# Attention in a one-core kernel: row sums by matmuls with ones behind the values product, in place of normalised probabilities

## The chip, the cores and the metric

The kernel runs on one core of one Trainium2 chip. A core has five engines with a queue each: TensorE (PE; its weight loads are PEld), VectorE (DVE), ScalarE (ACT), GpSimd (POOL) and SyncE (SP, which only issues transfers here). The metric is the time of one execution on the device, in microseconds; lower is better.

## The reference

Four blocks on an input of 16 images of 28 x 28 pixels with 32 channels, each behind a group normalisation with a residual: windowed attention, a state-space block, a triangle product and a recurrent net. The change touches the first. Cut to what matters:

```python
win = x.reshape(B, nH, 7, nW, 7, C)...reshape(-1, 49, C)     # 256 windows of 49 pixels
qkv = win @ w_qkv + b_qkv                                     # 4 heads of 8 channels
attn = einsum('whnd,whmd->whnm', q, k) * scale
attn = softmax(attn, axis=-1)
out = einsum('whnm,whmd->whnd', attn, v)
out = out @ w_proj + b_proj
```

## The kernel before, in words

The 128 partitions hold four image groups (g, 32 channels each). Pixels lie along the free axis and are cut into 16 strips of 7 rows, 196 pixels, that is four windows of 49. A strip goes through attention in a software pipeline, and each engine has a function that writes one turn s of it: `pe_att`, `act_att`, `dve_att` and `pool_att`. Turns run from -1 to 17; the middle ones are loops of two turns. Every engine works in its own order, and semaphores join them: `x_r` counts finished instructions of kind x.

In turn s of the kernel before:

- TensorE: scores of strip s in two halves of two groups (L1150), queries and keys of strip s+1 (L1165, L1166), four groups of transposes of strip s-1's probabilities (L1193), the projection of strip s-2 (L1175), values of strip s+1 (L1234), the product of probabilities and values of strip s-1 (L1204, "values product").
- VectorE: for each half of the scores of strip s the row maxima (L1814) and their subtraction (L1820); the residual addition of strip s-2 (L1826); the row sums of the four groups (L1832) with two reciprocals (L1836).
- ScalarE: queries and keys out of PSUM (L701, L706), transposed blocks out of PSUM (L715) alternating with the exponentials (L724), values (L746), the values product out of PSUM with the bias of the values (L755).
- GpSimd: the strip of input by windows (L469), the keys masked by head (L474), and the multiplication of the four groups of exponentials by the reciprocals (L480), for which the transposes wait (`pn_r`).

Transposed blocks and values share two banks of PSUM in turn (`ring_r`); the values product has bank 7, queries, keys and projection share bank 4.

Behind turn 10 VectorE takes the statistics of the first two images, behind turn 11 ScalarE takes a logarithm and an exponential for their normalisation, and behind turn 12 VectorE writes them into padded images. On TensorE the first convolution of the state-space block comes between turns 15 and 16, and pieces of that block stand between, and behind, the parts of turns 16 and 17 (`early`, `late`); on VectorE turn 17 stands behind the block's first instruction (L1879).

Of the kernel before, what the change touches and what calls it, by code (L numbers as in the profile page):

```python
# [8 lines left out]
ALU = mybir.AluOpType  # L9
# [29 lines left out]
def build(nc, a, out):  # L39
    ctx = ExitStack()  # L40
    with ctx:
# [26 lines left out]
        epsc = sb("epsc", [P, 1])  # L68
        early_ln = sb("early_ln", [P, 1])
        negone = sb("negone", [P, 1])  # L70
        vec = sb("vec", [P, 16])
# [46 lines left out]
        mx = sb("mx", [P, G, 8], att)  # L118
        sm = sb("sm", [P, G, 8], att)
        rc = sb("rc", [P, G, 8], att)  # L120
        att.close()
# [88 lines left out]
        qk_d, v_r, s_r, t_r, av_r, pj_r, q_r, k_r, exp_r, ring_r = sems("qk_d v_r s_r t_r av_r pj_r q_r k_r exp_r ring_r")  # L210
        xw_r, km_r, pn_r, max_r, sub_r, sum_r, rec_r, ao_r, x1_r = sems("xw_r km_r pn_r max_r sub_r sum_r rec_r ao_r x1_r")

# [28 lines left out]
        def windows(ap):  # L241

            return ap.rearrange("p (r w c) -> p w r c", r=WS, w=NW)

        def bcast(ap, axis, n):
# [186 lines left out]
        def _(eng):  # L432
# [27 lines left out]
            def pool_att(s, par):  # L460
                nxt = not isinstance(s, int) or s + 1 < NS
                cur = not isinstance(s, int) or s >= 0
                np_ = 1 - par
                if nxt:
# [197 lines left out]
        def _(eng):  # L662
# [28 lines left out]
            def act_att(s, par, before_output=None):  # L691
# [3 lines left out]
                prv = not fixed or 1 <= s <= NS  # L695
                np_ = 1 - par
                if nxt:
# [11 lines left out]
                def turned_out(g):  # L709
                    if not prv:  # L710
                        return
                    eng.wait_ge(t_r, 4 * (s - 1) + g + 1)
                    if g == 0 and (not fixed or s >= 2):
                        eng.wait_ge(av_r, s - 1)
                    eng.activation(PT[:, g].rearrange("p a b (o q) -> p (a b o) q", o=2),  # L715
                                   banks[5 + (par + 1 + g) % 2][:, :].rearrange("p (m k) -> p m k", k=WP)[:, :, 0:WT], ACT.Copy).then_inc(ring_r, 1)

                def exponent(g):
                    if not cur:
                        return  # L720
                    eng.wait_ge(sub_r, 4 * s + g + 1)
                    if not fixed or s >= 2:
                        eng.wait_ge(t_r, 4 * (s - 2) + g + 1)
                    eng.activation(Pr[:, par, g, :, 0:WT], Ts[:, g, :, :], ACT.Exp).then_inc(exp_r, 1)  # L724
# [390 lines left out]
        def _(eng):  # L1115
# [13 lines left out]
            def pe_att(s, par, early=None, late=None):  # L1129
# [25 lines left out]

                scores(0)
                scores(1)
                if nxt:
                    if fixed and s < 0:
                        eng.wait_ge(s_xn, J)  # L1160
                    else:
                        eng.wait_ge(k_r, s + 1)
                    if not fixed or s >= 3:
                        eng.wait_ge(x1_r, s - 2)
                    eng.matmul(banks[4][:, 0:ST], BD[:, U_Q, :], XN[:, strip(s + 1)], start=True, stop=True)  # L1165
                    eng.matmul(banks[4][:, ST:2 * ST], BD[:, U_K, :], XN[:, strip(s + 1)], start=True, stop=True).then_inc(qk_d, 1)  # L1166

                def project():
# [12 lines left out]
                def transposes(g):  # L1181
                    eng.wait_ge(pn_r, 4 * (s - 1) + g + 1)

# [12 lines left out]
                def av():  # L1196
# [4 lines left out]
                    for w in range(NW):  # L1201
                        for e in range(2):
                            for g in range(G):
                                ins = eng.matmul(banks[7][C * g:C * g + C, WT * w:WT * w + WT], Vst[:, np_, w % 2, w // 2, g, e, :],  # L1204
                                                 PT[:, g, w // 2, e, WT * (w % 2):WT * (w % 2) + WT],
                                                 start=(e == 0), stop=(e == 1))
                    ins.then_inc(av_r, 1)

                if prv:
                    transposes(0)  # L1210
                    transposes(1)
                if early:
                    early()
# [7 lines left out]
                if fixed and s < 0:  # L1221

                    eng.wait_ge(s_v, TRB)
                    for g in range(G):
                        rows = slice(C * g, C * g + C)
                        eng.matmul(banks[7][rows, 0:C], NB[0:R, 17, :], TB[0:R, 16, :], start=True, stop=True)
                        ins = eng.matmul(banks[7][rows, C:C + 1], wzn[:, :], lnb[:, :], start=True, stop=True)
                    ins.then_inc(s_wd, 1)
                if nxt:
# [468 lines left out]
        def _(eng):  # L1698
# [8 lines left out]
            eng.memset(negone[:, :], -1.0)  # L1707
            eng.memset(epsc[:, :], EPS).then_inc(s_ev, 1)

            for j in range(0, J, 2):  # L1710
# [92 lines left out]
            def dve_att(s, par):  # L1803
# [4 lines left out]
                np_ = 1 - par  # L1808
                if cur:
                    for part in range(2):  # L1810
                        groups = (2 * part, 2 * part + 1)
                        eng.wait_ge(s_r, 2 * s + part + 1)
                        for g in groups:
                            eng.tensor_reduce(mx[:, g, :], banks[g][:, 0:392].rearrange("p (m k) -> p m k", k=WT), AX.X,  # L1814
                                              ALU.max).then_inc(max_r, 1)
                        for g in groups:
                            eng.wait_ge(max_r, 4 * s + g + 1)
                            if not fixed or s >= 1:
                                eng.wait_ge(exp_r, 4 * (s - 1) + g + 1)
                            eng.tensor_tensor(Ts[:, g, :, :], banks[g][:, 0:392].rearrange("p (m k) -> p m k", k=WT),  # L1820
                                              bcast(mx[:, g, :], 2, WT), ALU.subtract).then_inc(sub_r, 1)
# [5 lines left out]
                if cur:  # L1827
                    for g in range(G):
                        eng.wait_ge(exp_r, 4 * s + g + 1)
                        if not fixed or s >= 1:  # L1830
# [399 lines left out]
```

## Time and profile before

| what | value |
|---|---|
| three runs | 471.02, 473.19, 474.92 us; median 473.19 us |
| profiled execution, span from first to last instruction | 473.1 us |
| instructions | 10122 |
| busy: PE, PEld, DVE, ACT, POOL | 358.7, 233.1, 366.5, 299.2, 233.8 us |
| DVE's maxima of turn 0 to those of turn 15 | 31.75 to 139.26 us |

The page gives no time of the profiled execution beside its span; the span stands here for it, and it is 0.1 us from the median of the runs. Busy time is summed over stages that have different limits, so it doesn't say which engine sets the end in attention. In a timeline, a line gives the start, the time from the start of the first to the end of the last instruction merged into it, engine, line, operation, destination and sources, the number of instructions, and in brackets how long the engine sat idle before it and what it waited for.

### The profile page before, as it was taken

Reading aid. Unit: us, or ns where it says so; the run is one execution under the profiler, and the core shown is the slowest. Engines: PE = TensorE matmul, PEld = TensorE weight load, DVE = VectorE, ACT = ScalarE, POOL = GpSimd, SP = SyncE. Lnnn points to the kernel's source line nnn. Section 1 sums busy time; section 2 is a strip of 40 time slices with the busy share of each in tenths; the row PEclk is TensorE's granted clock in tenths of the full one; section 3 lists DMA queues with packets and bytes.
Section 4 is the critical chain, followed back from the end, with each engine's and each line's share of the span. In section 5 each row is a group of like instructions: output and inputs, shape, how many; then the busy total and the mean of one; then the engine's idle time right before and its main releaser. Section 6 shows DMA issues by size and latency. Waiting matters only on the chain. (4 is left out here: it accounts for less than half of the span.)

```text
span 473.1 us, 10122 instructions
## 1 busy us (share of the span) xinstructions
PE 358.7 (76%) x3531; PEld 233.1 (49%) x3531; DVE 366.5 (77%) x679; ACT 299.2 (63%) x583; POOL 233.8 (49%) x217
## 2 busy tenths in 40 slices
PE   4159888896789785996767565567797989888885
PEld 4047666675665432142223222122295549877774
DVE  4799999999697388789698899999575895544443
ACT  4327788887785899568775976344996354333432
POOL 4527868775663224964893799587162240000000
PEclk9557999998899999588898896766999999999999
DMA  6110000000222231013000000000002000111111
GB/s 148 5 18 3 4 0 0 0 0 1 55 63 66 55 86 31 1 35 82 1 0 1 0 1 0 0 0 1 1 10 62 0 1 11 20 19 22 21 19 26
DMA packets 24045, 10.31 MB, mean 22 GB/s; under 512 B 20576, under 2 KB 22368, under 8 KB 24016
## 3 DMA queue, kind: packets, MB, share of 16 engines
q1 hardware_dynamic: 23888, 9.93, 10.3%
q8 instruction: 16, 0.26, 0.2%
q0 software_dynamic: 128, 0.01, 0.2%
q14 instruction: 13, 0.11, 0.1%
HBM read 2.00 MB, written 1.61 MB: 8 GB/s over the span
## 5 line engine op out<-in xcount | busy, mean ns | idle before, releaser
L480 POOL TENSOR_TENSOR Pr<-Pr,rc 128x392 f32<-128x392 f32 x64 | 54.3, 881 | 32.5 <-DVE rc L1836 32.5
L511 POOL TENSOR_TENSOR YA<-YA,hC 128x784 f32<-128x784 f32 x27 | 52.8, 1956 | 34.4 <-DVE hC L1920 33.3
L1349 PE MATMUL pair<-BCf,sel 96*128 96x392 bf16 x128 | 38.0, 391 | 32.4 <-DVE Hs L1904 28.9
L1904 DVE TENSOR_TENSOR_SCAN Hs<-dA,pair 128x784 f32<-128x784 f32 x32 | 57.1, 1785 | 1.0
L1193 PE MATMUL pair<-ident,Pr 128*128 128x128 f32 x256 | 41.3, 294 | 13.2 <-ACT PT L715 8.7
L1349 PEld LDWEIGHTS pair<-BCf,sel 96*128 96x128 bf16 x128 | 10.3, 104 | 71.8 <-issue 70.2
L1193 PEld LDWEIGHTS pair<-ident,Pr 128*128 128x128 f32 x256 | 29.5, 147 | 25.1 <-ACT PT L715 15.9
L1897 DVE TENSOR_TENSOR pair<-DU,pair 128x784 f32<-128x784 f32 x32 | 31.2, 974 | 10.9 <-PE pair L1349 10.5
L715 ACT ACTIVATE PT<-pair 128x392 f32<-128x392 f32 x64 | 31.3, 496 | 6.2 <-PE pair L1193 5.9
L724 ACT ACTIVATE Pr<-Ts 128x392 f32<-128x392 f32 x64 | 32.5, 536 | 3.3 <-DVE Ts L1820 3.2
L1814 DVE TENSOR_REDUCE mx<-pair 128x8 f32<-128x392 f32 x64 | 32.6, 551 | 1.3 <-PE pair L1150 1.0
L1646 PE MATMUL pair<-hst,BD 128*128 128x112 f32 x168 | 25.7, 289 | 10.1 <-DVE hst L2193 9.2
L1820 DVE TENSOR_TENSOR Ts<-pair,mx 128x392 f32<-128x392 f32 x64 | 32.9, 555 | 0.0
L846 ACT ACTIVATE dA<-DL,Aneg 128x784 f32<-128x784 f32 x32 | 29.0, 940 | 5.2 <-DVE Hs L1904 5.1
L1832 DVE TENSOR_REDUCE sm<-Pr 128x8 f32<-128x392 f32 x64 | 31.9, 538 | 0.3 <-ACT Pr L724 0.3
L2180 DVE SCALAR_TENSOR_TENSOR prods<-gates 128x112 f32<-128x112 f32 x28 | 7.7, 276 | 31.5 <-ACT gates L1100 31.5
L1100 ACT ACTIVATE gates<-pair 128x224 f32<-128x224 f32 x28 | 10.0, 357 | 33.7 <-PE pair L1646 33.7
L474 POOL TENSOR_TENSOR Km<-Ks,mask 128x784 f32<-128x784 f32 x16 | 24.1, 1505 | 11.9 <-ACT Ks L706 11.9
L1920 DVE TENSOR_TENSOR hC<-Hs,pair 128x784 f32<-128x784 f32 x27 | 25.7, 951 | 3.3 <-PE pair L1349 3.2
L1646 PEld LDWEIGHTS pair<-hst,BD 128*128 128x128 f32 x168 | 20.9, 191 | 14.7 <-DVE hst L2193 14.3
L1287 PE MATMUL pair<-SX,W 96*32 96x392 f32 x192 | 22.7, 588 | 6.1 <-ACT BCf L815 5.6
L746 ACT ACTIVATE Vst<-pair 64x128 f32<-64x128 f32 x64 | 17.3, 271 | 15.1 <-PE pair L1204 8.6
(262 smaller groups left out, 943.2 us busy)
## 6 DMA issues: line engine op xcount, KB each, us to landing
SX<-XP SPq DMA_DIRECT2D x48, 112.2 KB
XT<-in_x SPq DMA_DIRECT2D x4, 392.0 KB, 5.1
out<-Os SPq DMA_DIRECT2D x28, 56.0 KB, 1.8
AD<-Aa SPq DMA_DIRECT2D x4, 196.0 KB
NB<-in_L_conv_x_proj_w SPq DMA_DIRECT2D x4, 3.0 KB
DW<-in_L_conv_dw SPq DMA_DIRECT2D x4, 1.1 KB
vec<-in_L_conv_b_qkv POOLq DMA_DIRECT2D x3, 0.5 KB, 5.8
W<-in_L_conv_w_qkv SPq DMA_DIRECT2D x1, 48.0 KB
```

Of the source, the lines that this page charges most:

```text
L480: eng.tensor_tensor(pg, pg, bcast(rc[:, g, :], 2, WT), ALU.mult).then_inc(pn_r, 1)
L511: eng.tensor_tensor(y, y, hC[:, n % NHC, :], ALU.add).then_inc(g_ya, 1)
L715: eng.activation(PT[:, g].rearrange("p a b (o q) -> p (a b o) q", o=2), banks[5 + (par + 1 + g) % 2][:, :].rearrange("p (m k) -> p m k", k ...
L724: eng.activation(Pr[:, par, g, :, 0:WT], Ts[:, g, :, :], ACT.Exp).then_inc(exp_r, 1)
L1193: ins = eng.transpose(bk[:, P * k:P * k + P], pg, ident[:, :])
L1349: ins = eng.matmul(SPREAD[s][:, columns(h)], sel[:, n, :], upper(BCf[:, c % 2, s, columns(h)]), start=True, stop=True)
L1646: ins = eng.matmul(zb[k], BD[:, U_M + k, :], hst[:, 1 - par, :], start=False, stop=True, skip_group_check=True)
L1814: eng.tensor_reduce(mx[:, g, :], banks[g][:, 0:392].rearrange("p (m k) -> p m k", k=WT), AX.X, ALU.max).then_inc(max_r, 1)
L1820: eng.tensor_tensor(Ts[:, g, :, :], banks[g][:, 0:392].rearrange("p (m k) -> p m k", k=WT), bcast(mx[:, g, :], 2, WT), ALU.subtract).then_ ...
L1832: eng.tensor_reduce(sm[:, g, :], Pr[:, par, g, :, 0:WT], AX.X, ALU.add).then_inc(sum_r, 1)
L1897: eng.tensor_tensor(SPREAD[0], DU[:, c % 2, :], SPREAD[0], ALU.mult).then_inc(v_b, 1)
L1904: eng.tensor_tensor_scan(Hs[:, n % 2, :], dA[:, n % NA, :], SPREAD[0], 0.0, ALU.mult, ALU.add).then_inc(v_s, 1)
```

## The change

The exponentials are transposed as they are. Behind the values product of strip s-1 TensorE multiplies the same transposed blocks by a matrix of ones (`ones`, set up at the start), which gives each pixel's sum of exponentials, per head, in the other half of bank 7, laid out as the values product is. VectorE inverts these 128x196 sums (`den`) and multiplies them into the values product on its way out of PSUM, one turn later (`attended`). That takes the place of VectorE's row sums and small reciprocals, GpSimd's multiplications and ScalarE's eviction of the values product. The bias of the values goes through the projection into the projection's bias, once at the start. The order within a turn changes as well: on TensorE the first group of transposes stands ahead of the scores, the second behind them and ahead of queries and keys; on ScalarE the first two transposed blocks stand ahead of queries and keys, and the exponentials behind all four blocks; on VectorE `attended` stands between the two halves of maxima and subtractions.

```diff
@@ pool_att
-                if cur:
-                    for g in range(G):
-                        eng.wait_ge(rec_r, 2 * s + g // 2 + 1)
-                        pg = Pr[:, par, g, :, 0:WT]
-                        eng.tensor_tensor(pg, pg, bcast(rc[:, g, :], 2, WT), ALU.mult).then_inc(pn_r, 1)
@@ act_att
+                turned_out(0)
+                turned_out(1)
                 if nxt:
                     eng.wait_ge(qk_d, s + 2)
...
-                turned_out(0)
-                exponent(0)
-                turned_out(1)
-                exponent(1)
                 turned_out(2)
                 turned_out(3)
-                exponent(2)
-                exponent(3)
+                for g in range(G):
+                    exponent(g)
...
-                if prv:
-                    eng.wait_ge(av_r, s)
-                    if not fixed or s >= 3:
-                        eng.wait_ge(pj_r, s - 2)
-                    eng.activation(windows(AO[:, np_, :]), banks[7][:, 0:ST].rearrange("p (w r c) -> p w r c", w=NW, r=WS),
-                                   ACT.Identity, bias=vec[:, V_BV:V_BV + 1]).then_inc(ao_r, 1)
@@ pe_att
                 def transposes(g):
-                    eng.wait_ge(pn_r, 4 * (s - 1) + g + 1)
+                    eng.wait_ge(exp_r, 4 * (s - 1) + g + 1)
...
                     ins.then_inc(av_r, 1)
+                    if fixed and s == 1:
+                        eng.wait_ge(ones_r, 3)
+                    for e in range(2):
+                        for g in range(G):
+                            ins = eng.matmul(banks[7][C * g:C * g + C, 256:256 + ST], ones[:, e, :], PT[:, g, :, e, :],
+                                             start=(e == 0), stop=(e == 1))
+                    ins.then_inc(sum_r, 1)
 
                 if prv:
                     transposes(0)
+                scores(0)
+                scores(1)
+                if prv:
                     transposes(1)
+                if nxt:
...
+                    eng.matmul(banks[4][:, 0:ST], BD[:, U_Q, :], XN[:, strip(s + 1)], start=True, stop=True)
+                    eng.matmul(banks[4][:, ST:2 * ST], BD[:, U_K, :], XN[:, strip(s + 1)], start=True, stop=True).then_inc(qk_d, 1)
                 if early:
                     early()
@@ setup
+            eng.memset(ones[:, :, :], 0.0).then_inc(ones_r, 1)
+            eng.wait_ge(ones_r, 1)
+            for u in range(2):
...
+                eng.memset(heads, 1.0).then_inc(ones_r, 1)
...
+                    eng.matmul(banks[7][:, C + 1:C + 2], BD[:, U_P, :], vec[:, V_BV:V_BV + 1], start=True, stop=True).then_inc(s_wd, 1)
...
+            eng.tensor_tensor(vec[:, V_BP:V_BP + 1], vec[:, V_BP:V_BP + 1], banks[7][:, C + 1:C + 2], ALU.add)
@@ dve_att
+                def attended():
+
+                    eng.wait_ge(sum_r, s - 1)
+                    eng.reciprocal(den[:, :], banks[7][:, 256:256 + ST]).then_inc(rec_r, 1)
+                    eng.wait_ge(rec_r, s - 1)
+                    eng.tensor_tensor(windows(AO[:, par, :]), by_window(banks[7][:, 0:ST]),
+                                      by_window(den[:, :]), ALU.mult).then_inc(ao_r, 1)
+
+                shifted(0)
                 if prv2:
-
+                    attended()
+                shifted(1)
+                if prv2:
                     eng.wait_ge(pj_r, s - 1)
                     xs = X[:, strip(s - 2)]
                     eng.scalar_tensor_tensor(xs, banks[4][:, 0:ST], vec[:, V_BP:V_BP + 1], xs, ALU.add, ALU.add).then_inc(x1_r, 1)
-                if cur:
-                    for g in range(G):
-                        eng.wait_ge(exp_r, 4 * s + g + 1)
-                        if not fixed or s >= 1:
-                            eng.wait_ge(pn_r, 4 * (s - 1) + g + 1)
-                        eng.tensor_reduce(sm[:, g, :], Pr[:, par, g, :, 0:WT], AX.X, ALU.add).then_inc(sum_r, 1)
-                        if g >= 2:
-                            lo = 2 * (g - 2)
-                            eng.wait_ge(sum_r, 4 * s + lo + 2)
-                            eng.reciprocal(rc[:, lo:lo + 2, :], sm[:, lo:lo + 2, :]).then_inc(rec_r, 1)
```

`shifted(part)` is the former first loop of `dve_att` for one half, unchanged: wait for that half of the scores, two maxima, two subtractions. The projection (`project`) is unchanged: it waits for `ao_r` to reach s-1, which `attended` of the same turn now counts; so does the values product, as before.

## Rows read from the trace of the kernel before

**Rows 1.** Busy time by stage: length, then each engine, then PEclk, DMA.

```profile
68.00:101.00 33.00, 29.78 (x610) 22.79 (x610) 32.09 (x76) 28.09 (x76) 24.68 (x30) 1.00 0.00 0
```

**Rows 2.** Timeline of VectorE in attention and behind it.

```profile
44.50 1.04 DVE L1814 TENSOR_REDUCE mx<-pair 128x8 f32<-128x392 f32 x2 [0.20 <-PE pair L1150]
...
58.30 1.04 DVE L1814 TENSOR_REDUCE mx<-pair 128x8 f32<-128x392 f32 x2 [0.53 <-PE pair L1150]
...
91.98 1.04 DVE L1814 TENSOR_REDUCE mx<-pair 128x8 f32<-128x392 f32 x2
...
93.89 1.03 DVE L1814 TENSOR_REDUCE mx<-pair 128x8 f32<-128x392 f32 x2
...
96.22 1.49 DVE L1832 TENSOR_REDUCE sm<-Pr 128x8 f32<-128x392 f32 x3
...
98.49 0.99 DVE L1814 TENSOR_REDUCE mx<-pair 128x8 f32<-128x392 f32 x2
...
114.36 1.04 DVE L1814 TENSOR_REDUCE mx<-pair 128x8 f32<-128x392 f32 x2
...
126.39 1.02 DVE L1814 TENSOR_REDUCE mx<-pair 128x8 f32<-128x392 f32 x2
...
139.26 0.97 DVE L1814 TENSOR_REDUCE mx<-pair 128x8 f32<-128x392 f32 x2
...
162.66 1.62 DVE L1879 SCALAR_TENSOR_TENSOR sp<-sp 128x784 f32<-128x784 f32 x1 [7.73 <-ACT sp L823]
```

**Rows 3.** Timeline of ScalarE behind turn 11 and at attention's end.

```profile
115.22 1.28 ACT L771 ACT_TABLE_LOAD   x1
...
118.23 0.41 ACT L701 ACTIVATE Qw<-pair,vec 128x196 f32<-128x196 f32 x1
...
157.77 0.44 ACT L755 ACTIVATE AO<-pair,vec 128x196 f32<-128x196 f32 x1 [0.28 <-PE pair L1204]
...
165.01 0.82 ACT L815 ACTIVATE BCf<-pair 96x784 f32<-96x784 f32 x1
```

**Rows 4.** Timeline of TensorE in attention.

```profile
57.34 0.95 PE L1150 MATMUL pair<-Km,Qw 32*64 32x196 f32 x32
...
90.65 1.11 PE L1150 MATMUL pair<-Km,Qw 32*64 32x196 f32 x32 [0.37 <-issue]
...
92.46 1.18 PE L1193 MATMUL pair<-ident,Pr 128*128 128x128 f32 x8
...
95.22 0.50 PE L1175 MATMUL pair<-AO,BD 128*128 128x196 f32 x2
95.56 0.69 PE L1234 MATMUL pair<-BD,xw 128*128 128x128 f32 x4
96.18 0.91 PE L1204 MATMUL pair<-PT,Vst 128*32 128x49 f32 x64
97.02 0.95 PE L1150 MATMUL pair<-Km,Qw 32*64 32x196 f32 x32
...
109.77 1.12 PE L1193 MATMUL pair<-ident,Pr 128*128 128x128 f32 x4 [1.93 <-ACT PT L715]
...
144.01 4.13 PE L1287 MATMUL pair<-SX,W 96*32 96x392 f32 x48
```

**Rows 5.** The page's costliest groups: count, busy us, mean ns, idle before.

```profile
L480 POOL TENSOR_TENSOR Pr<-Pr,rc 128x392 f32<-128x392 f32 x64 | 54.3, 881 | 32.5 <-DVE rc L1836 32.5
...
L1820 DVE TENSOR_TENSOR Ts<-pair,mx 128x392 f32<-128x392 f32 x64 | 32.9, 555 | 0.0
```

**Rows 6.** Reciprocals by line: duration ns min/median/max, first and last start.

```profile
L1836 DVE RECIPROCAL rc<-sm x32: 234/248/254, 36.9 to 145.5; 128x16 f32<-128x16 f32 x32
...
L2099 DVE RECIPROCAL zst<-zst x4: 271/317/319, 367.6 to 373.0; 128x28 f32<-128x28 f32 x4
...
L1951 DVE RECIPROCAL rstd<-lnv x3: 156/157/164, 324.4 to 343.1; 128x1 f32<-128x1 f32 x2, 128x2 f32<-128x2 f32 x1
```

**Rows 7.** Busy time in half microseconds where TensorE had idled; PEclk third from the end.

```profile
109.50:110.00 0.50, 0.23 (x1) 0.23 (x2) 0.50 (x2) 0.50 (x2) 0.08 (x1) 0.50 0.00 0
```

More of the change, by code:

```diff
@@ L69, in build @@
         early_ln = sb("early_ln", [P, 1])
+        ones = sb("ones", [P, 2, C])
         negone = sb("negone", [P, 1])
@@ L118, in build @@
         mx = sb("mx", [P, G, 8], att)
-        sm = sb("sm", [P, G, 8], att)
-        rc = sb("rc", [P, G, 8], att)
+        den = sb("den", [P, ST], att)
         att.close()
@@ L210, in build @@
         qk_d, v_r, s_r, t_r, av_r, pj_r, q_r, k_r, exp_r, ring_r = sems("qk_d v_r s_r t_r av_r pj_r q_r k_r exp_r ring_r")
-        xw_r, km_r, pn_r, max_r, sub_r, sum_r, rec_r, ao_r, x1_r = sems("xw_r km_r pn_r max_r sub_r sum_r rec_r ao_r x1_r")
+        xw_r, km_r, max_r, sub_r, sum_r, ln_r, rec_r, ao_r, x1_r, ones_r = sems("xw_r km_r max_r sub_r sum_r ln_r rec_r ao_r x1_r ones_r")
         PRODUCTS = "conv x2 u z delta xB xC out var wout".split()
@@ L243, in windows, with by_window @@
             return ap.rearrange("p (r w c) -> p w r c", r=WS, w=NW)
+        def by_window(ap):
+            return ap.rearrange("p (v y c) -> p v y c", v=NW, y=WS)
         def bcast(ap, axis, n):
@@ L461, in pool_att @@
                 nxt = not isinstance(s, int) or s + 1 < NS
-                cur = not isinstance(s, int) or s >= 0
                 np_ = 1 - par
@@ L696, in act_att, with turned_out, exponent @@
                 np_ = 1 - par
+                def turned_out(g):
+                    if not prv:
+                        return
+                    eng.wait_ge(t_r, 4 * (s - 1) + g + 1)
+                    if g == 0 and (not fixed or s >= 2):
+                        eng.wait_ge(sum_r, s - 1)
+                    eng.activation(PT[:, g].rearrange("p a b (o q) -> p (a b o) q", o=2),
+                                   banks[5 + (par + 1 + g) % 2][:, :].rearrange("p (m k) -> p m k", k=WP)[:, :, 0:WT], ACT.Copy).then_inc(ring_r, 1)
+                def exponent(g):
+                    if not cur:
+                        return
+                    eng.wait_ge(sub_r, 4 * s + g + 1)
+                    if not fixed or s >= 2:
+                        eng.wait_ge(t_r, 4 * (s - 2) + g + 1)
+                    eng.activation(Pr[:, par, g, :, 0:WT], Ts[:, g, :, :], ACT.Exp).then_inc(exp_r, 1)
+                turned_out(0)
+                turned_out(1)
                 if nxt:
@@ L708, in act_att @@
                                    bias=vec[:, V_BK:V_BK + 1]).then_inc(k_r, 1)
[L709 to L724, printed above, removed]
-                turned_out(0)
-                exponent(0)
-                turned_out(1)
-                exponent(1)
                 turned_out(2)
                 turned_out(3)
-                exponent(2)
-                exponent(3)
+                for g in range(G):
+                    exponent(g)
                 if nxt:
@@ L1154, in scores @@
                     ins.then_inc(s_r, 1)
[L1156 to L1166, printed above, removed]
                 def project():
@@ L1207, in av @@
                     ins.then_inc(av_r, 1)
+                    if fixed and s == 1:
[5 more added lines that the diff above has]
+                    ins.then_inc(sum_r, 1)
                 if prv:
                     transposes(0)
+                scores(0)
+                scores(1)
+                if prv:
                     transposes(1)
+                if nxt:
+                    if fixed and s < 0:
+                        eng.wait_ge(s_xn, J)
+                    else:
+                        eng.wait_ge(k_r, s + 1)
+                    if not fixed or s >= 3:
+                        eng.wait_ge(x1_r, s - 2)
+                    eng.matmul(banks[4][:, 0:ST], BD[:, U_Q, :], XN[:, strip(s + 1)], start=True, stop=True)
+                    eng.matmul(banks[4][:, ST:2 * ST], BD[:, U_K, :], XN[:, strip(s + 1)], start=True, stop=True).then_inc(qk_d, 1)
                 if early:
@@ L1226, in pe_att @@
                         eng.matmul(banks[7][rows, 0:C], NB[0:R, 17, :], TB[0:R, 16, :], start=True, stop=True)
-                        ins = eng.matmul(banks[7][rows, C:C + 1], wzn[:, :], lnb[:, :], start=True, stop=True)
-                    ins.then_inc(s_wd, 1)
+                        eng.matmul(banks[7][rows, C:C + 1], wzn[:, :], lnb[:, :], start=True, stop=True)
+                    eng.matmul(banks[7][:, C + 1:C + 2], BD[:, U_P, :], vec[:, V_BV:V_BV + 1], start=True, stop=True).then_inc(s_wd, 1)
                 if nxt:
@@ L1708, in _ @@
             eng.memset(epsc[:, :], EPS).then_inc(s_ev, 1)
+            eng.memset(ones[:, :, :], 0.0).then_inc(ones_r, 1)
+            eng.wait_ge(ones_r, 1)
+            for u in range(2):
+                half = ones[64 * u:64 * u + 64]
+                heads = bass.AP(half.tensor, half.offset + HD * u, [list(half.ap[0]), [C + 2 * HD, 2], [1, HD]])
+                eng.memset(heads, 1.0).then_inc(ones_r, 1)
             for j in range(0, J, 2):
@@ L1808, in dve_att, with shifted @@
                 np_ = 1 - par
-                if cur:
[L1810 to L1817, printed above, removed]
-                            if not fixed or s >= 1:
-                                eng.wait_ge(exp_r, 4 * (s - 1) + g + 1)
-                            eng.tensor_tensor(Ts[:, g, :, :], banks[g][:, 0:392].rearrange("p (m k) -> p m k", k=WT),
-                                              bcast(mx[:, g, :], 2, WT), ALU.subtract).then_inc(sub_r, 1)
+                def shifted(part):
+                    if not cur:
+                        return
+                    groups = (2 * part, 2 * part + 1)
+                    eng.wait_ge(s_r, 2 * s + part + 1)
+                    for g in groups:
+                        eng.tensor_reduce(mx[:, g, :], banks[g][:, 0:392].rearrange("p (m k) -> p m k", k=WT), AX.X,
+                                          ALU.max).then_inc(max_r, 1)
+                    for g in groups:
+                        eng.wait_ge(max_r, 4 * s + g + 1)
+                        if not fixed or s >= 1:
+                            eng.wait_ge(exp_r, 4 * (s - 1) + g + 1)
+                        eng.tensor_tensor(Ts[:, g, :, :], banks[g][:, 0:392].rearrange("p (m k) -> p m k", k=WT),
+                                          bcast(mx[:, g, :], 2, WT), ALU.subtract).then_inc(sub_r, 1)
+                def attended():
+                    eng.wait_ge(sum_r, s - 1)
+                    eng.reciprocal(den[:, :], banks[7][:, 256:256 + ST]).then_inc(rec_r, 1)
[6 more added lines that the diff above has]
+                shifted(1)
                 if prv2:
@@ L1826, in dve_att @@
                     eng.scalar_tensor_tensor(xs, banks[4][:, 0:ST], vec[:, V_BP:V_BP + 1], xs, ALU.add, ALU.add).then_inc(x1_r, 1)
-                if cur:
-                    for g in range(G):
-                        eng.wait_ge(exp_r, 4 * s + g + 1)
-                        if not fixed or s >= 1:
-                            eng.wait_ge(pn_r, 4 * (s - 1) + g + 1)
-                        eng.tensor_reduce(sm[:, g, :], Pr[:, par, g, :, 0:WT], AX.X, ALU.add).then_inc(sum_r, 1)
-                        if g >= 2:
-                            lo = 2 * (g - 2)
-                            eng.wait_ge(sum_r, 4 * s + lo + 2)
-                            eng.reciprocal(rc[:, lo:lo + 2, :], sm[:, lo:lo + 2, :]).then_inc(rec_r, 1)
             for s in (0, 1, 2):
```

## The prediction

> **What bounds the kernel now.** I read the stage table first, then VectorE's timeline of one turn, then TensorE's, then the few places where attention is not in its steady turn. The stage table [rows 1] shows VectorE busy 32.09 of 33.00 us in the steady part of attention, TensorE 29.78, ScalarE 28.09 and GpSimd 24.68. VectorE's timeline says the same in detail: within a turn (maxima, subtractions, residual, row sums, reciprocals) each instruction starts as the one before ends, and the next turn's maxima follow with hardly a gap; turn 9 runs from 91.98 to 98.49, 6.51 us [rows 2]. So in the steady turns VectorE is the bound, and the row sums with their reciprocals, 96.22 to 98.49, are 2.27 us of it. TensorE spends that time on the values product and the next scores, so it has the next maxima's input ready about when VectorE comes free.
>
> Two stretches differ. The turn that starts at 114.36 takes 12.03 us, because ScalarE loads activation tables from 115.22 until its next query eviction at 118.23 [rows 2, 3]. And attention's end releases the rest: the first convolution starts on TensorE at 144.01, straight after the last steady turn [rows 4], and the state-space part starts from that. I therefore take a shift of attention's end as a shift of the whole.
>
> **What is removed.** Of VectorE, 2.27 us a turn (four sums, two reciprocals). Of GpSimd, 64 multiplications of 881 ns [rows 5]: they sat between the sums and the transposes, and GpSimd is not the bound; without them the transposes need the exponentials alone, which a turn earlier are long done. Of ScalarE, one eviction of 0.44 us a turn [rows 3]; ScalarE has room.
>
> **What is added.** (a) The reciprocal of 128x196. No row has one so long. Reciprocals of 16 elements take 248 ns, of 28 elements 317, of one or two 157 [rows 6]: 317 - 248 over 12 is 5.8 ns an element, 248 - 157 over 14 is 6.5. I take 6.0 ns on 248 for 16: 0.248 + 180 x 0.0060 = 1.33 us. The ends: 7.0 ns (156 to 254 over 14 elements) gives 1.51 us; a plain instruction's rate, a 128x392 subtraction in 555 ns [rows 5] and so half its elements in some 0.36, is the floor. I stand near the first, since it is the same operation.
>
> The Trainium skill ("VectorE: DVE Perf Modes", section "Walkthrough: the 8-slice pipeline in each mode") says that the reciprocal is an iterative divide with a repeat count of 8. Read as eight cycles an element at the page's 0.96 GHz that is an estimate of 8.3 ns, 1.75 us for 196 elements, and would put the total 6 us above mine; the rows' 5.8 to 6.5 ns do not bear that out.
>
> (b) The multiplication of 128x196: half the elements of a subtraction, 0.36 us. It waits for the reciprocal's end, 0.05 more. VectorE's new step is 1.33 + 0.05 + 0.36 = 1.74 us.
>
> (c) The matmuls with ones: eight of 196 columns into four column groups. The values product in front has 32 of 49 columns into the same groups, so as many columns (1568), and holds TensorE from 96.18 to 97.02, 0.84 us [rows 4]; with an eighth to a quarter of the weight loads I take 0.75, between 0.5 and 0.84. If the groups did not overlap it were sixteen passes of some 0.17 (a projection, two passes, holds TensorE 0.34, 95.22 to 95.56), 2.7 us. It can't be below zero: the work is new.
>
> Setup: one memset with its two strips at the start, where VectorE waits for x, one 128x1 addition, one one-column matmul: 0.2 us together, inside the rounding.
>
> **What is moved, and the loop that it closes.** VectorE's total per turn falls: 6.51 - 2.27 + 1.74 = 5.98 us. But the new step stands between the two halves of the maxima, and on TensorE the projection, in order, waits for it; behind the projection are queued the next values (V), the values product, the sums, the first transposes and only then the next scores; and for those scores VectorE's next maxima wait, before which the next new step cannot come. Before, the projection's input came from ScalarE at the end of the turn before, and no such round existed. It, once a turn:
>
> - start of scores to the first maximum: 57.34 to 58.30 with VectorE idle, 0.96 [rows 2, 4];
> - both maxima and subtractions of the first half: 91.98 to 93.89, 1.91;
> - reciprocal and multiplication, 1.74;
> - hand-over to TensorE with the projection's weight load, 0.15 (estimate; TensorE's hand-overs in these rows are that or more);
> - projection, V, values product: 95.22 to 97.02, 1.80;
> - sums, 0.75;
> - the first transposes, now ahead of the scores: two groups take 1.18 [rows 4], of which a matmul's own latency is part; 0.55.
>
> Sum 7.86 us, against 5.98 of VectorE's work. TensorE then idles about a microsecond before each projection and VectorE nearly two before the scores come. I checked the other rounds: keys to mask to scores (GpSimd's mask, no longer queued behind multiplications), and ScalarE's order (transposed blocks, queries, keys, blocks, four exponentials, values) end earlier than this one.
>
> **The sum.** Turns 2 to 14, from the maxima at 44.50 to those at 139.26, took 94.76 us [rows 2]. After: 13 x 7.86 = 102.2; six loop boundaries at which TensorE idles 0.37 [rows 4], now on the round, 2.2; the statistics after turn 10 0.3 (2.2 us of them into 1.9 of slack); the two table loads 0.4, because ScalarE's 3 us now fall where the projection waits anyway. Together 105.1, +10.3 us. Turns 0 and 1: VectorE is lighter by the sums, but TensorE at 1.2 GHz does transposes and sums more before the next scores: worked out at the rows' durations, +0.6. End of the last steady turn: 144.01 - 139.26 = 4.75 before; after, 1.91 + 1.74 + 0.15 + 0.34 + 0.84 + 0.75 = 5.7, +1.0. The tail: ScalarE's last output eviction at 157.77 with 0.28 of idle before it falls away, -0.7 [rows 3]; but the last new step is queued on VectorE behind the instruction at 162.66 (1.62 us) of the state-space part, and the last projection, the product that ScalarE evicts at 165.01 and the second convolution are queued behind it on TensorE: 162.63 + 1.67 + 1.74 + 0.15 + 0.34 + 1.5 (that product) = 168.0, +3.0 [rows 2, 3]. Net +2.3.
>
> 0.6 + 10.3 + 1.0 + 2.3 = +14.2 us. The profiled execution's span, 473.1, agrees with the median of 473.19, so I put the sum on the median: 487. By the bounds: the reciprocal at 1.11 or 1.51 moves it by -3 or +3 (15 times), the sums at 0.5 or 0.84 by -4 or +1, the hand-overs and the tail by some 3 either way. Own range 478 to 497.
>
> **Rivals.**
> 1. The reciprocal costs like any other instruction, 0.36. The round shrinks by 0.97 in 15 turns: 487 - 14.6 = 472.5, no change. Against it: rows 6. Chance 0.10.
> 2. Faster: the round does not bind, and VectorE stays the bound. It turns on the round being under VectorE's 6 us: that takes a reciprocal of 0.36 and another microsecond less, as where the first half of the scores releases the maxima after 0.5 (not 0.96, which the rows show with both halves in flight) and the sums hide half their time. Then turns of 6.2 and loop boundaries give 13 x 6.2 + 2.2 + 0.7 = 83.5, -11.2, with the other terms at +1: 463. Chance 0.07.
> 3. TensorE's clock falls. Before, TensorE idled 1.93 us up to 109.77, and the granted clock went from 1.00 to 0.50 (2.4 to 1.2 GHz) at that point; one group of transposes there took 1.12 us, where two take 1.18 at the full clock [rows 1, 4, 7]. The changed kernel idles about 1 us in every turn; shorter gaps left the clock alone before. If half of the turns fell to 1.2 GHz behind the wait, each would pay about 1.5 us more: 487 + 10 = 497. Chance 0.13; matmuls with ones that don't overlap (+27) are in it with 0.02.
>
> **How the numbers follow.** The forecast has 0.70, with the rivals 0.10, 0.07 and 0.13. 1% is 4.7 us, about what a measurement of this kernel can tell from no change. Slower by more: nearly all of the forecast and of rival 3, 0.80. Within: rival 1 and the forecast's low edge, 0.12. Faster: 0.08, rival 2 and rival 1's low edge. The range takes the forecast's own and reaches down to the edge of rival 1 and up to rival 3: 474 to 498.
>
> **What would show it.** VectorE's instruction on a 128x196 reciprocal at 1.1 to 1.5 us. Turns of 7.6 to 8.2 us in place of 6.7. The projection waiting on VectorE's multiplication, about 1 us a turn, as TensorE's longest wait, and VectorE's first maxima waiting for the scores, near 2 us. VectorE's busy share in this stage down to about three quarters. The convolution starting some 12 us later, with the state-space part unchanged but for its start. It would be wrong if the reciprocal runs at plain speed, or if the turn is shorter than the sum of its round, which would mean that a hand-over is sooner than the rows show.

## The result and the profile after

The changed kernel takes 482.91 us (median of five, 482.28 to 486.42) where the kernel before took 473.19 beside it (five, 470.89 to 474.92): a ratio of 1.024 [1.019, 1.028], 9.7 us slower. The forecast was 487 in a range of 474 to 498, with 0.80 on slower. The profiled execution of the changed kernel is the slowest of its five: 486.42 us at a span of 483.5; the spans of the others are 480.1 to 481.6. Positions below are those of that profile.

The stage table over the same stretch of attention as [rows 1] (same columns):

```profile
68.00:101.00 33.00, 25.64 (x562) 20.48 (x560) 25.15 (x48) 22.86 (x61) 7.68 (x9) 1.00 0.00 0
```

Every engine is less busy than before, VectorE 25.15 us in place of 32.09, and yet less attention is done in these 33 us. No engine bounds this stretch any more. One turn on VectorE, from the timeline (start, busy us, line, names, count, and in brackets the idle time ahead and what ended it); it answers to the turn in [rows 2]:

```profile
67.01 1.04 DVE L1818 TENSOR_REDUCE mx<-pair 128x8 f32<-128x392 f32 x2 [1.93 <-PE pair L1138]
67.96 1.03 DVE L1824 TENSOR_TENSOR Ts<-pair,mx 128x392 f32<-128x392 f32 x2
68.91 1.38 DVE L1830 RECIPROCAL den<-pair 128x196 f32<-128x196 f32 x1
70.32 0.36 DVE L1832 TENSOR_TENSOR AO<-pair,den 128x196 f32<-128x196 f32 x1
70.60 1.03 DVE L1818 TENSOR_REDUCE mx<-pair 128x8 f32<-128x392 f32 x2
71.54 1.03 DVE L1824 TENSOR_TENSOR Ts<-pair,mx 128x392 f32<-128x392 f32 x2
72.48 0.42 DVE L1842 SCALAR_TENSOR_TENSOR X<-pair,vec,X 128x196 f32 x1
74.83 1.04 DVE L1818 TENSOR_REDUCE mx<-pair 128x8 f32<-128x392 f32 x2 [1.93 <-PE pair L1138]
```

The same turn on TensorE, which answers to [rows 4]:

```profile
66.05 0.95 PE L1138 MATMUL pair<-Km,Qw 32*64 32x196 f32 x32
...
68.08 1.04 PE L1169 MATMUL pair<-ident,Pr 128*128 128x128 f32 x8
70.81 0.59 PE L1151 MATMUL pair<-AO,BD 128*128 128x196 f32 x2 [1.69 <-DVE AO L1832]
71.24 0.61 PE L1229 MATMUL pair<-BD,xw 128*128 128x128 f32 x4
71.78 0.91 PE L1180 MATMUL pair<-PT,Vst 128*32 128x49 f32 x64
72.51 0.84 PE L1188 MATMUL pair<-PT,ones 128*32 128x196 f32 x16
73.28 0.66 PE L1169 MATMUL pair<-ident,Pr 128*128 128x128 f32 x4
73.87 0.95 PE L1138 MATMUL pair<-Km,Qw 32*64 32x196 f32 x32
```

Read the two brackets together. VectorE stands idle 1.93 us until the scores (L1138) come; the scores are last in TensorE's queue; TensorE stands idle 1.69 us until VectorE's multiplication (L1832); and that multiplication is behind the first maxima, for which those scores are the input. Two engines wait for each other once a turn, 7.82 us from maxima to maxima. The table of waits over attention (engine, line, waited for: us in total, times, longest) has the two waits side by side:

```profile
PE pair L1151 <- DVE AO L1832: 20.3, 12, 1.8
DVE mx L1818 <- PE pair L1138: 20.3, 11, 1.9
```

### The profile page after: what moved, and what is told of

The parts are those of the page before. It is cut to its first block and busy times, and to the rows that moved or that the text cites. A ratio compares the mean times of both kernels' runs of the same rounds, so it can differ in the third digit from the quotient of the medians.

```text
span 483.5 us, 10400 instructions
## 1 busy us (share of the span) xinstructions
PE 361.7 (75%) x3789; PEld 236.9 (49%) x3789; DVE 352.2 (73%) x619; ACT 295.0 (61%) x567; POOL 179.1 (37%) x153
## 5 line engine op out<-in xcount | busy, mean ns | idle before, releaser
L508 POOL TENSOR_TENSOR YA<-YA,hC 128x784 f32<-128x784 f32 x27 | 51.7, 1914 | 32.8 <-DVE hC L1926 32.0
L1344 PEld LDWEIGHTS pair<-BCf,sel 96*128 96x128 bf16 x128 | 10.4, 104 | 71.5 <-issue 69.5
L709 ACT ACTIVATE Pr<-Ts 128x392 f32<-128x392 f32 x64 | 31.5, 549 | 20.3 <-DVE Ts L1824 20.3
L1169 PE MATMUL pair<-ident,Pr 128*128 128x128 f32 x256 | 37.8, 281 | 3.2 <-ACT PT L700 2.0
L1903 DVE TENSOR_TENSOR pair<-DU,pair 128x784 f32<-128x784 f32 x32 | 31.2, 974 | 10.3 <-PE pair L1344 9.8
L700 ACT ACTIVATE PT<-pair 128x392 f32<-128x392 f32 x64 | 30.1, 501 | 12.4 <-PE pair L1169 12.0
L1151 PE MATMUL pair<-AO,BD 128*128 128x196 f32 x32 | 9.9, 391 | 27.6 <-DVE AO L1832 27.6
L1282 PE MATMUL pair<-SX,W 96*32 96x392 f32 x192 | 23.7, 611 | 5.3 <-ACT BCf L803 5.3
L1629 PE MATMUL pair<-XN,BD 128*128 (+1 forms) x168 | 25.2, 287 | 1.8 <-ACT XN L1068 1.8
L493 POOL TENSOR_TENSOR BCf<-BCf 64x784 f32<-64x784 f32 x8 | 11.9, 1487 | 32.8 <-ACT BCf L803 32.8
```

What stands on the lines that cost most here:

```text
L508: eng.tensor_tensor(y, y, hC[:, n % NHC, :], ALU.add).then_inc(g_ya, 1)
L1169: ins = eng.transpose(bk[:, P * k:P * k + P], pg, ident[:, :])
L1344: ins = eng.matmul(SPREAD[s][:, columns(h)], sel[:, n, :], upper(BCf[:, c % 2, s, columns(h)]), start=True, stop=True)
L1629: eng.matmul(zb[k].rearrange("p (b n) -> p b n", b=J), BD[:, U_X + k, :], xt, start=False, stop=False, skip_group_check=True)
L1903: eng.tensor_tensor(SPREAD[0], DU[:, c % 2, :], SPREAD[0], ALU.mult).then_inc(v_b, 1)
```

## Experiments

The leading theory: the changed step costs time because of its place. It stands between the two halves of the maxima, and so closes the round; neither VectorE's total nor the matmuls with ones bound the turn by themselves. Its rival: the step's own work (a long reciprocal on VectorE, sixteen more matmuls on TensorE) is what costs, wherever it stands. All edits are made to the changed kernel.

**The product ahead of the maxima.** The same instructions, but the reciprocal and the multiplication are issued ahead of the first half instead of behind it.

```diff
-                shifted(0)
                 if prv2:
                     attended()
+                shifted(0)
                 shifted(1)
```

> Moves the reciprocal and the multiplication on VectorE ahead of both halves of the maxima; no work is taken away. Theory (the round through the scores, the first maxima, the reciprocal and the projection sets the turn, 7.82 us in the trace of the changed kernel): the projection no longer waits for this turn's maxima, TensorE's wait of 1.69 us goes, and the turn falls to TensorE's own work, 6.1 to 6.3 us; 14 turns by some 1.6 make it about 22 us faster than the changed kernel, about 461 us and below the kernel before. Rival (the added work itself, the matmuls with ones and the long reciprocal, costs the time): nothing is removed, so the time stays within 3 us of 483.

Measured: 465.11 us (461.82 to 467.41), 0.984 [0.978, 0.990] of the kernel before and 17.8 us under the changed one, with no instruction fewer. The turn is 6.23 us, reciprocal to reciprocal, on VectorE's timeline of this kernel:

```profile
62.85 1.38 DVE L1830 RECIPROCAL den<-pair 128x196 f32<-128x196 f32 x1 [0.34 <-PE pair L1188]
64.27 0.36 DVE L1832 TENSOR_TENSOR AO<-pair,den 128x196 f32<-128x196 f32 x1
64.55 1.03 DVE L1818 TENSOR_REDUCE mx<-pair 128x8 f32<-128x392 f32 x2
65.49 1.02 DVE L1824 TENSOR_TENSOR Ts<-pair,mx 128x392 f32<-128x392 f32 x2
66.44 1.02 DVE L1818 TENSOR_REDUCE mx<-pair 128x8 f32<-128x392 f32 x2
67.38 1.02 DVE L1824 TENSOR_TENSOR Ts<-pair,mx 128x392 f32<-128x392 f32 x2
68.33 0.41 DVE L1842 SCALAR_TENSOR_TENSOR X<-pair,vec,X 128x196 f32 x1
69.08 1.38 DVE L1830 RECIPROCAL den<-pair 128x196 f32<-128x196 f32 x1 [0.34 <-PE pair L1188]
```

The maxima no longer wait for scores: while VectorE inverts and multiplies, TensorE already does them. What is left of idle time is 0.34 us before the reciprocal, for the sums. What sets this turn is TensorE's own matmuls, which follow each other almost without a gap (stage table of this kernel):

```profile
68.00:101.00 33.00, 32.81 (x758) 25.69 (x754) 31.12 (x60) 28.50 (x76) 9.44 (x12) 1.00 0.00 0
```

So the rival falls: the same work in another place is faster than the kernel before. The time missed its expectation by 4 us, and the trace says where. In the turn with the table loads the reciprocals start at 107.74 and 117.81, 10.07 us apart, where that turn took 8.13 in the changed kernel: ScalarE's loads are on the path again, since nothing else waits there. TensorE's timeline of this kernel shows the wait for ScalarE's transposed block:

```profile
112.78 1.36 PE L1169 MATMUL pair<-ident,Pr 128*128 128x128 f32 x8 [2.33 <-ACT PT L700]
...
115.60 1.48 PE L1180 MATMUL pair<-PT,Vst 128*32 128x49 f32 x64
```

Behind it the granted clock is 0.82 over 112.50 to 114.00, after 1.00 over 107 to 113, and the values product takes 1.48 us instead of 0.91.

**The reciprocal and the multiplication left out.** One copy in their place, so the output stays unnormalised.

```diff
-                    eng.reciprocal(den[:, :], banks[7][:, 256:256 + ST]).then_inc(rec_r, 1)
-                    eng.wait_ge(rec_r, s - 1)
-                    eng.tensor_tensor(windows(AO[:, par, :]), by_window(banks[7][:, 0:ST]),
-                                      by_window(den[:, :]), ALU.mult).then_inc(ao_r, 1)
+                    eng.tensor_copy(windows(AO[:, par, :]), by_window(banks[7][:, 0:ST])).then_inc(ao_r, 1)
```

> Leaves out the reciprocal and the multiplication: the unnormalised values product is copied out of PSUM by VectorE in the same place (about 0.3 us in place of 1.77). The sums are still made and not used. Theory: the round shrinks by 1.4 to 1.5 us to some 6.35, about 20 us faster than the changed kernel. Rival (TensorE's added matmuls are what lengthens the turn): VectorE had 1.9 us of idle time in the turn already, so no more than 3 us.

Measured: 464.81 us (459.61 to 466.00), 0.980 [0.972, 0.988] of the kernel before. VectorE's timeline of this kernel:

```profile
62.54 1.04 DVE L1818 TENSOR_REDUCE mx<-pair 128x8 f32<-128x392 f32 x2 [1.93 <-PE pair L1138]
...
64.44 0.35 DVE L1830 COPY AO<-pair 128x196 f32<-128x196 f32 x1
...
68.94 1.04 DVE L1818 TENSOR_REDUCE mx<-pair 128x8 f32<-128x392 f32 x2 [1.93 <-PE pair L1138]
```

The turn is 6.40 us, shorter by 1.42: the reciprocal's 1.38 and its hand-over to the multiplication. VectorE idles 1.93 us as before. So in the changed place each microsecond of the reciprocal is a microsecond of the turn, although VectorE has room for it. The turn came out as expected (6.35); the time is 18.1 us under the changed kernel instead of about 20. The time lies near that of the product first by chance: there TensorE's matmuls set a turn of 6.23 us, here the round sets one of 6.40.

**More work for VectorE off the round.** Three row sums a turn (of the shifted scores) are put back on VectorE behind its last instruction of the turn, where it waits for scores. The sums are used nowhere.

```diff
...
+                if cur:
+                    for g in range(3):
+                        eng.wait_ge(sub_r, 4 * s + g + 1)
+                        eng.tensor_reduce(sm[:, g, :], Ts[:, g, :, :], AX.X, ALU.add)
```

> Puts three row sums of 128x392 (of the shifted scores, results unused) back on VectorE behind the residual addition, 1.45 us a turn. Theory: they fit into VectorE's idle 1.93 us before the next maxima, so the turn stays at 7.8 us and the time within 2 us of the changed kernel: the row sums that the change removed are worth nothing in its own turn. Rival (VectorE's work sets the turn in the changed kernel too): 14 times 1.45, 20 us slower.

In the steady turns this held: 7.82 us (maxima at 68.07 and 75.89) with 1.48 us more on VectorE a turn, taken from the 1.93 of idle. In VectorE's timeline of this kernel:

```profile
73.87 1.48 DVE L1847 TENSOR_REDUCE sm<-Ts 128x8 f32<-128x392 f32 x3
75.89 1.04 DVE L1819 TENSOR_REDUCE mx<-pair 128x8 f32<-128x392 f32 x2 [0.54 <-PE pair L1139]
...
112.97 1.48 DVE L1847 TENSOR_REDUCE sm<-Ts 128x8 f32<-128x392 f32 x3
114.38 1.96 DVE L1721 BATCH_NORM_STATS2 stats<-X 128x6 f32<-128x392 f32 x4
116.37 0.28 DVE L1862 BATCH_NORM_AGGREGATE mv<-stats 128x2 f32<-128x12 f32 x2
116.57 0.98 DVE L1819 TENSOR_REDUCE mx<-pair 128x8 f32<-128x392 f32 x2
...
118.42 1.37 DVE L1831 RECIPROCAL den<-pair 128x196 f32<-128x196 f32 x1
```

But the whole took 488.78 us (487.20 to 492.55), 5.9 more than the changed kernel against at most 2 expected. The lower lines show why: after turn 10 the statistics (2.2 us) follow, and with the sums ahead of them the slack of 1.93 is used twice. The next maxima start at 116.57 with no idle time ahead, and the reciprocal comes 9.35 us after the last one (109.07 to 118.42), where the changed kernel has 7.95. The late product then makes TensorE wait, in its timeline of this kernel:

```profile
120.31 1.01 PE L1152 MATMUL pair<-AO,BD 128*128 128x196 f32 x2 [3.22 <-DVE AO L1833]
```

The granted clock is 0.50 over 120.50 to 122.50, and the turn that follows takes 10.45 us (118.42 to 128.87) instead of 7.83. The same happens once more, smaller, before 139.16. Slack in the steady turn is not slack in every turn.

**The last product taken earlier.** Only the last product is moved on VectorE, ahead of the state-space part's instruction of 1.62 us (line 1885 of the changed kernel); the round stays as it is. `rest=False` leaves out the residual addition of the turn, `product=False` the reciprocal and the multiplication.

```diff
...
+            dve_att(17, 1, rest=False)
             eng.wait_ge(a_u, 1)
             eng.scalar_tensor_tensor(rest, sp[:, SP_U, :], 1.0, sp[:, SP_E, :], ALU.subtract, ALU.subtract).then_inc(v_cc, 1)
-            dve_att(17, 1)
+            dve_att(17, 1, product=False)
```

> Only the last strip's reciprocal and multiplication move, on VectorE, ahead of the state-space part's first instruction. Theory of the tail: TensorE's idle 5.46 us before the last projection falls to about 1, the projection and the product behind it run at full clock, and ScalarE's copy of that product no longer waits 4.77 us; 4 to 5 us faster at the first scan, of which 3 to 5 reach the end. Rival (the first scan waits for other work of the tail): under 1 us.

Measured: 477.61 us (475.87 to 479.28), 5.3 under the changed kernel. First the changed kernel, TensorE's timeline at the last product:

```profile
173.39 1.02 PE L1151 MATMUL pair<-AO,BD 128*128 128x196 f32 x2 [5.46 <-DVE AO L1832]
174.21 2.82 PE L1267 MATMUL pair<-US,WBC 128*96 128x392 f32 x4
```

and this kernel:

```profile
169.18 0.60 PE L1151 MATMUL pair<-AO,BD 128*128 128x196 f32 x2 [0.41 <-DVE AO L1832]
169.62 1.48 PE L1267 MATMUL pair<-US,WBC 128*96 128x392 f32 x4
```

Without the 5.46 us of waiting TensorE keeps its clock (1.00 over 169 to 172, where the changed kernel has 0.50 over 173.50 to 176.50), and the product for ScalarE's copy takes 1.48 us instead of 2.82. The copy itself starts at 173.21 instead of 177.12, and the first scan at 182.02 instead of 185.96. The profiled execution of this kernel is 1.06 us late before the edit comes into play (turn 15's maxima at 146.72 instead of 145.66), so from there the first scan comes 5.0 us sooner, 35.30 us in place of 40.30. The 5.3 us are a little more than the expected 3 to 5 at the end.

**Both moves together.** The product ahead of the maxima and the last one early.

> Both moves together: reciprocal and multiplication ahead of the maxima in every turn, and the last strip's ahead of the state-space part's first instruction. Theory: the two places are apart in time, so the gains add: 465.1 less about 5, some 460 us, and clearly below both kernels. Rival (the tail's gain was only the clock's, or is hidden once attention is shorter): within 2 us of 465.

Measured: 463.04 us (458.84 to 463.28), 0.975 [0.971, 0.979]: faster than both kernels, 10.4 us under the one before and 19.9 under the changed one. The expected 460 was not reached. Of the second move 2 us are left here by the medians (465.11 to 463.04) and some 4 by the two ratios (0.984 and 0.975), whose intervals touch: that the gains add is not shown. Its trace has the first scan 6.3 us earlier than the kernel with the product first alone (162.41 and 168.70); 1.1 of them are there at the first convolution already (134.24 and 135.36), ahead of the second move, and 5.2 come at it. The recurrence's first input is only 1.9 earlier (379.02 and 380.88). Between the first scan and that input, where neither edit changes anything, this kernel takes 216.61 us and the one without the second move 212.18.

**Only the reciprocal ahead of the maxima.** The multiplication stays between the halves.

```diff
...
+                if prv2:
+                    inverted()
                 shifted(0)
                 if prv2:
                     attended()
```

> Only the reciprocal moves ahead of the maxima; the multiplication stays between the two halves and the projection still waits for it. Theory: the round loses the reciprocal's 1.41 us, as the reciprocal fits between the end of the sums and the arrival of the scores (1.5 us), so the turn is 6.4 us, as without any reciprocal, and the time 463 to 468 us. Rival (a reciprocal costs its time wherever it stands): the turn stays at 7.8 and the time at 483.

Measured: 466.64 us (465.74 to 468.40), 0.984 [0.979, 0.989]. VectorE's timeline of this kernel:

```profile
69.77 1.38 DVE L1830 RECIPROCAL den<-pair 128x196 f32<-128x196 f32 x1 [0.52 <-PE pair L1188]
71.18 1.04 DVE L1818 TENSOR_REDUCE mx<-pair 128x8 f32<-128x392 f32 x2
...
73.08 0.35 DVE L1835 TENSOR_TENSOR AO<-pair,den 128x196 f32<-128x196 f32 x1
...
76.18 1.38 DVE L1830 RECIPROCAL den<-pair 128x196 f32<-128x196 f32 x1 [0.52 <-PE pair L1188]
```

6.41 us a turn, as expected. The sums are ready while VectorE waits for scores, so the reciprocal fits into that wait and the round loses 1.4 us, as it did when the reciprocal was left out. That tells the reciprocal's place from its cost without taking anything away.

**The sums left out.** The matmuls with ones are removed and the reciprocal reads the values product instead, so the output is not attention's. VectorE's wait for the sums, and one of ScalarE's, become waits for the values product.

```diff
-                    for e in range(2):
-                        for g in range(G):
-                            ins = eng.matmul(banks[7][C * g:C * g + C, 256:256 + ST], ones[:, e, :], PT[:, g, :, e, :],
-                                             start=(e == 0), stop=(e == 1))
-                    ins.then_inc(sum_r, 1)
...
-                    eng.wait_ge(sum_r, s - 1)
-                    eng.reciprocal(den[:, :], banks[7][:, 256:256 + ST]).then_inc(rec_r, 1)
+                    eng.wait_ge(av_r, s - 1)
+                    eng.reciprocal(den[:, :], banks[7][:, 0:ST]).then_inc(rec_r, 1)
```

> Leaves out the matmuls with ones; the reciprocal takes the values product itself, at the same size and place, so that the output is not the attention's. Theory: the sums stand on the round with 0.77 us, the turn falls to 7.05 and the time by 14 to 15 times that, to 470 to 473 us. Rival (TensorE has 1.69 us of idle time in each turn that would take the sums up): the time stays within 3 us of 483.

Measured: 476.70 us (474.18 to 478.46), 6.2 under the changed kernel: short of the expected 470 to 473, and more than the rival's 3. VectorE's timeline of this kernel:

```profile
65.30 1.04 DVE L1813 TENSOR_REDUCE mx<-pair 128x8 f32<-128x392 f32 x2 [1.63 <-PE pair L1138]
...
72.45 1.04 DVE L1813 TENSOR_REDUCE mx<-pair 128x8 f32<-128x392 f32 x2 [1.26 <-PE pair L1138]
...
79.99 1.04 DVE L1813 TENSOR_REDUCE mx<-pair 128x8 f32<-128x392 f32 x2 [1.65 <-PE pair L1138]
```

The turns alternate, 7.15 and 7.54. In the changed kernel every turn is 7.82. A turn without the sums is 0.67 shorter, but every second one pays 0.39 at the loop boundary, as TensorE did before (0.37, [rows 4]). With the sums that boundary costs nothing. My reading is that the sums hold TensorE for 0.77 us with sixteen instructions, where the values product has sixty-four in 0.73, so that its queue is full again before it is needed; this last step is argued, not shown.

## Why the prediction was right, and where its sizes were off

**The round** came out as worked out, 7.82 us against 7.86. By its parts, from the two timelines above, predicted and measured: scores to first maxima 0.96 and 0.96; first half 1.91 and 1.90; reciprocal and multiplication 1.74 and 1.77; hand-over 0.15 and 0.13; projection, V and values product 1.80 and 1.70; sums 0.75 and 0.77; first transposes 0.55 and 0.59. The two predicted waits are there, but longer than said on TensorE's side (1.69 instead of about 1).

**The reciprocal** takes 1.38 us, between its bounds of 1.11 and 1.51 (the rows give the upper one; the lower had no working). From 16 elements [rows 6] to 196 that is (1.375 - 0.248) / 180 = 6.3 ns an element. The Trainium skill ("VectorE: DVE Perf Modes", section "Walkthrough: the 8-slice pipeline in each mode"), read as eight cycles an element, gave an estimate of 1.75; the trace disagrees, and the short rows were the better guide.

**Loop boundaries** were the term most mis-sized in the steady turns. I put 2.2 us on six of them, because TensorE's 0.37 would lie on the round; it measured 0, and the last experiment shows that the 0.37 returns when the sums are taken out. With that, turns 2 to 14 took 102.04 us (43.62 to 145.66) against 105.1 predicted: +7.3 instead of +10.3. The table loads did sink into the waits (that turn 8.13 us, before 12.03 [rows 2]), as predicted.

**Turns 0 and 1** gave -0.9 instead of +0.6: turn 2's first maxima start at 43.62, at 44.50 before. That is within what executions differ by: two kernels with the same code up to there have 43.42 (reciprocal left out) and 44.73 (last product early). **The end of the last steady turn** took 6.14 us from maxima to convolution (145.66 to 151.80), +1.4 instead of +1.0. TensorE's timeline of the changed kernel there:

```profile
149.39 0.60 PE L1151 MATMUL pair<-AO,BD 128*128 128x196 f32 x2 [1.85 <-DVE AO L1832]
149.91 0.91 PE L1180 MATMUL pair<-PT,Vst 128*32 128x49 f32 x64
150.65 1.40 PE L1188 MATMUL pair<-PT,ones 128*32 128x196 f32 x16
151.80 5.34 PE L1282 MATMUL pair<-SX,W 96*32 96x392 f32 x48
```

The granted clock over 149.50 to 151.50 is 0.82; the sums take 1.40 us where they take 0.84 in the steady turn, and the convolution's 48 matmuls 5.34 where they took 4.13 [rows 4].

**The tail** cost more than its +2.3. The convolution starts 7.8 us later than before, ScalarE's copy 12.1 (165.01 in [rows 3], now 177.12), so +4.3 came there. The queue named was the right one, VectorE's line 1885 ahead of the last product, and moving the product past it gave 5.3 us back. What the term lacked was the clock: the wait of 5.46 us on TensorE is followed by matmuls at half speed, 2.82 us where I counted 1.5.

**What came back.** The first scan starts 12.1 us later than before and the recurrence's first input 9.4, since the state-space stretch between them takes 213.89 us where it took 216.67. The edit changes nothing there. The same stretch differs between the kernels of this study, and TensorE's clock differs in it. In the slice from 50 to 60 us behind the first scan the granted clock is 0.74 in the kernel before (216.67 us), 0.75 with both moves (216.61), 0.83 in the changed kernel (213.89), 1.00 with the product first alone (212.18) and 1.00 with the last product early alone (211.68). In the slice from 10 to 20 us the order is less clear: 0.71, 0.70, 0.80, 0.82 and 0.80. So the kernel with both moves gave back 4.4 of the 6.3 us that it was ahead of the one with the product first; that is not the second move's doing, since by itself it goes with the shortest stretch. Each of these lengths is that of one execution, and executions of one kernel differ by as much (461.82 to 467.41 us with the product first). The windows of the slice from 50 to 60 us, first with both moves (first scan at 162.41),

```profile
212.41:222.41 10.00, 7.83 (x32) 3.08 (x30) 6.21 (x7) 6.72 (x8) 9.05 (x6) 0.75 0.00 0
```

then with the product first alone (first scan at 168.70),

```profile
218.70:228.70 10.00, 7.45 (x56) 2.22 (x54) 9.16 (x9) 9.92 (x12) 9.92 (x7) 1.00 0.00 0
```

and with the last product early alone (first scan at 182.02):

```profile
232.02:242.02 10.00, 7.54 (x54) 2.22 (x54) 9.16 (x9) 9.92 (x11) 9.92 (x7) 1.00 0.00 0
```

So of the distance between +14.2 and +9.7 some 3 us came back in a stretch that the change does not touch and that the prediction had put at no change. Why the clock falls there as it does, and whether it alone makes the length, stays open; no run here isolates it.

**The sum.** -0.9, +7.3, +1.4 and +4.3 make the +12.1 us at the first scan, against +14.2; the -2.8 behind it leaves +9.4 (rounded) at the recurrence, and the two profiled spans end 10.4 apart. Against the prediction the terms miss by -1.5, -3.0, +0.4, +2.0 and -2.8. They partly cancel, so that the total lies only 4 us from 487 is in part luck; the length of the turn is not.

**The rivals.** A reciprocal at plain speed (472.5) did not occur. VectorE stayed the bound in no steady turn of the changed kernel; in the one with the statistics alone its next maxima follow without idle time (114.12), which makes it 8.01 us long. The kernel that has the product first has nearly the rival's turn (6.23 where it said 6.2), and its 465 lies near the rival's 463, but for another reason: TensorE's matmuls bound it. The mechanism was right and the place in the program decided it. The falling clock (497) occurred not in the steady turns but in two places at attention's end, behind idle times of 1.85 and 5.46 us: 0.6 us more on the sums, 1.2 on the convolution, 0.4 on the last projection (1.02 against 0.60) and 1.3 on the product behind it.

## What to carry to other kernels

Before counting what an edit takes off an engine, follow the new step's output back to its own input: where the consumer is queued on another engine ahead of the work that releases the producer's next turn, the round's sum is the turn, as long as no engine's own work is longer. A step whose input is ready early belongs ahead of what waits, not in the middle of it; here moving one call was worth 18 us, more than the 10 that the change cost. And slack that a steady turn shows is to be checked in the turns that carry extra work, as the three added sums showed.

## What was not expected of the hardware

Eight matmuls with ones in sixteen passes of 196 columns, into four groups of columns, hold TensorE 0.77 us at the full clock; a projection of two passes of 196 columns holds it 0.43 in the same turn (70.81 to 71.24). Sixteen at that rate would take 3.4 us, so the groups must run beside each other. The granted clock was 1.00 over 68 to 101 us of the changed kernel, with 1.69 us of idle time in every turn, and fell behind a single 1.85 us; but in the kernel without the sums it was 1.00 behind idle times of 2.15 and 2.33 us (windows 113.50 to 115.50 and 120.50 to 122.50), and 0.82 behind 2.33 us where the product comes first. The length of one gap alone does not tell whether the clock falls behind it.
